# A decoder layer on one core: transposes by DMA, score maxima inside the product, two tanh gates, and every engine's order written out

## The reference

```
x = x + attention(layernorm(x))       # 16 query heads in 4 groups of 4, 4 key/value heads of 16, rope, causal softmax
x = x + cross(layernorm(x), ctx)      # scores over 256 features with ctx, mask of keys, softmax, readout of ctx
x = x + ffn(layernorm(x))             # 256 -> 2 x 704 -> 256
# ffn: every row of x, w_gate_up, h and w_down is rounded to 127 steps of its largest magnitude
gate_up = xq @ w1q.T;  h = silu(gate) * up;  y = quant(h) @ w2q.T
```

## Time and profile before

| what | value |
| --- | --- |
| median of 3 runs | 142.97 us (140.73 to 143.29) |
| span of the profiled execution | 146.3 us; the page gives no other time of that execution |
| busiest engine over the span | PE 124.6 us, 85% |
| granted TensorE clock, mean | 0.820 of full speed |
| DMA packets and bytes | 7281, 6.97 MB |

### The profile page before, as it was taken

How to read it: one execution, slowest core, us unless ns; L and a number is a source line. 1 busy time by engine, 2 the same in 40 slices (tenths; PEclk the granted TensorE clock), 3 DMA queues, 4 the chain that set the end, 5 groups by cost and what they waited for, 6 DMA issues and landing times.

```text
span 146.3 us, 2608 instructions
## 1 busy us (share of the span) xinstructions
PE 124.6 (85%) x730; PEld 95.8 (65%) x730; DVE 96.7 (66%) x392; ACT 73.3 (50%) x179; POOL 44.8 (31%) x81
## 2 busy tenths in 40 slices
PE   0899739969979999999999999679889999994770
PEld 0676527757856896858687876558777877782330
DVE  4997969754943346776767345543599999969421
ACT  4012152932645435767583635538777876683200
POOL 3405071210312210322310212130664656666111
PEclk9999995999855558999999555557999999998555
DMA  1799801010010002010101010100000011001211
GB/s 51 189 347 331 309 1 40 0 36 0 0 36 4 2 2 72 2 36 0 36 0 36 4 36 6 30 0 0 0 0 7 0 36 36 23 20 36 72 36 36
DMA packets 7281, 6.97 MB, mean 48 GB/s; under 512 B 1185, under 2 KB 7014, under 8 KB 7270
## 3 DMA queue, kind: packets, MB, share of 16 engines
q1 hardware_dynamic: 7270, 6.84, 15.0%
HBM read 5.79 MB, written 1.05 MB: 47 GB/s over the span
## 4 chain that ended last, share of the span: by engine, by line
PE 63%; DVE 19%; issue 6%; ACT 4%; POOL 3%; DMA 1%; POOLq 1%; DVEq 0%; ACTq 0%; SPq 0%
PE ps_s L372 5%; PE bank L389 5%; PE bank L426 5%; PE ps_s L528 5%; PE bank L346 4%; PE bank L528 4%; PE bank L562 4%; PE bank L380 4%; PE bank L401 3%; PE bank L439 3%; PE bank L337 3%; PE bank L329 3%; POOL hid L1466 2%; PE bank L412 2%; PE bank L414 2%
## 5 line engine op out<-in xcount | busy, mean ns | idle before, releaser
L1466 POOL TENSOR_TENSOR hid<-gate,up 128x704 f32<-128x704 f32 x8 | 13.6, 1697 | 14.9 <-ACT up L808 14.9
L337 PE MATMUL bank<-causal,ident_b 128*128 128x256 bf16 x82 | 14.1, 322 | 4.2 <-DVE ident_b L916 4.1
L1434 POOL TENSOR_SCALAR w_q<-w_int,w_scale 128x256 f32<-128x256 int16 x11 | 5.2, 480 | 34.2 <-ACT w_int L726 34.2
L337 PEld LDWEIGHTS bank<-causal,ident_b 128*128 128x128 bf16 x82 | 9.2, 115 | 6.5 <-DVE ident_b L916 4.1
L562 PE MATMUL bank<-w_T,h_T 128*128 128x256 bf16 (+1 forms) x48 | 9.3, 323 | 4.1 <-DVE h_T L1246 4.0
L666 ACT COPY xn_T<-bank 128x256 f32<-128x256 f32 x8 | 3.0, 373 | 16.9 <-PE bank L321 16.9
L1425 POOL TENSOR_SCALAR ln_var<-x_sumsq 128x1 f32<-128x1 f32 x8 | 1.5, 191 | 29.2 <-ACT x_square L702 29.2
L528 PE MATMUL ps_s<-w_hi,x_int_T 128*128 128x352 f32 x32 | 9.1, 369 | 1.2 <-ACT x_int_T L792 1.2
L329 PE MATMUL bank<-ident,w_q 128*128 128x128 f32 x22 | 5.3, 330 | 5.7 <-DVE w_lo L1083 3.4
L1062 DVE SCALAR_TENSOR_TENSOR resid<-bank,c_factor,resid 128x256 f32 (+1 forms) x8 | 3.9, 484 | 9.5 <-PE bank L439 9.5
L389 PEld LDWEIGHTS bank<-v_ones,p_self_T 128*128 128x128 f32 x64 | 9.9, 230 | 0.3 <-issue 0.3
(11 more groups left out here) (149 smaller groups left out, 340.8 us busy)
## 6 DMA issues: line engine op xcount, KB each, us to landing
x_in<-in_x SPq DMA_DIRECT2D x8, 128.0 KB, 2.2
resid<-in_x SPq DMA_DIRECT2D x1, 1024.0 KB, 7.6
ctx_sb<-in_ctx SPq DMA_DIRECT2D x8, 128.0 KB, 2.1
out_x<-resid SPq DMA_DIRECT2D x8, 128.0 KB, 1.7
w_raw<-in_L_ffn_w_gate_up SPq DMA_DIRECT2D x1, 896.0 KB, 8.3
w_raw<-in_L_ffn_w_down SPq DMA_DIRECT2D x1, 704.0 KB, 8.3
w_raw<-in_L_ffn_w_gate_up SPq DMA_DIRECT2D x1, 512.0 KB, 4.4
wq_raw<-in_L_attn_Wq SPq DMA_DIRECT2D x1, 256.0 KB, 2.6
```

The source lines that it names most:

```text
L337: nc.tensor.matmul(ps_xc[:, 0:2 * T], ident_b[:, :], causal[:, :, :], start=True, stop=True)
L1466: nc.gpsimd.tensor_tensor(hid[par][:, :].rearrange("p (i f) -> p i f", i=2), gate[par][:, :, :], up[par][:, :, :], ALU.mult).then_inc(s["h ...
```

## The change

The kernel is written anew, with the same arithmetic in its outline. What is different:

- **Layout.** The host lays out x, its transpose, the context and its transpose, weights and rope tables by partition (`laid_out`: reshapes, transposes, copies of constants). The transposes of x (L321) and of the context (L414) fall away. SP and ACT issue the loads.
- **Norm 1 is folded into weights.** The mean is subtracted from the weights' columns (`mean_w_first`, `centre_w_first`), and the row factor r1 multiplies after the product, so x itself is the operand. The bias is added after rope on POOL (`rope_bias`, `rotate_c`, `rotate_sum`), while DVE does one operation per batch (`rotate`).
- **Maximum in the product.** Scores are computed once to find the row maxima (`scores`, `max_scores`); the negated maximum is written beside the 16 features of q as a 17th, q is transposed again (`transpose_q_max`), and a second set of products (`score_keys`) gives scores less the maximum, already transposed. Exponentials are taken from PSUM; POOL sets later keys to 0 (`drop_later_keys`). The transposes of probabilities (L380) and the subtraction (L998) fall away.
- **Values in column tiles.** Four products of 32 output rows each with the probabilities as moving operand (128 columns), and four more with ones for the sums (`weigh_values`); the result is already transposed.
- **Integers for up.** The up half stays in integers (one part, 4 products instead of 8); its scale is a row that POOL multiplies into the gate (`widen_gate`). The gate half keeps two parts, and its lower part is made by POOL (`lower_gate`).
- **Transposes by DMA.** w1, w2, x of batches 0 to 5 and h of batches 0 to 2 are transposed as 2-byte numbers by DMA from SP. The others go through TensorE.
- **Gate by tanh for batches 0 and 1** (`tanh_gate`, `finish_gate` on DVE), silu for the others.
- **Cross bias on POOL** (`bias_cross`), context centred on POOL (`centre_ctx`).
- **The end.** The last batch is cut in halves (`last_gate` to `last_down_b`).
- **All orders laid out.** No loops or slots: one list of steps for each engine. After the start no `keep_warm` is left (54 in all, 82 before).

```diff
-                nc.vector.tensor_reduce(s_negmax[:, :].rearrange("p (b h) -> p b h", b=2), scores, AX.X, ALU.max, negate=True).then_inc(s["negmax_done"], 1)
-                nc.vector.tensor_tensor(by_bank(s_shifted[:, :, :]), scores, by_bank(broadcast(s_negmax[:, :], T)), ALU.add).then_inc(s["shifted_ready"], 1)
-                    last = nc.tensor.transpose(ps_p[:, h * T:(h + 1) * T], p_self[par][:, h, :], ident[:, :])
-                    last = nc.tensor.matmul(ps_y[:, h * (DH + 1):(h + 1) * (DH + 1)], p_self_T[:, h, :],
-                                            v_ones[par][:, h, :], start=True, stop=True)
+                    nc.tensor.matmul(ps_s[:, h, 0:T], qk_T[j % 3][h * HP:h * HP + DH, 0, :],
+                                     qk_T[j % 3][h * HP:h * HP + DH, 1, :], start=False, stop=True).then_inc(s["scores_done"], 1)
+                nc.vector.tensor_reduce(qk_rot[j % 3][:, 0, :, DH], ps_s[:, :, 0:T], AX.X, ALU.max, negate=True).then_inc(s["negmax_done"], 1)
+                nc.tensor.transpose(ps_qm, qk_rot[j % 3][:, 0], ident[:, :]).then_inc(s["q_max_transposed"], 1)
+                    nc.tensor.matmul(ps_s[:, h, 0:T], qk_T[j % 3][h * HP:(h + 1) * HP, 1, :],
+                                     q_max_T[j % 3][h * HP:(h + 1) * HP, :], start=True, stop=True).then_inc(s["keys_done"], 1)
+                nc.scalar.activation(p_self_T[j % 3][:, :, :], ps_s[:, :, 0:T], ACT.Exp).then_inc(s["p_T_ready"], 1)
+                    nc.tensor.matmul(ps_yv[h * HP:(h + 1) * HP, :], v_pad[:, j, h, :], p_self_T[j % 3][:, h, :],
+                                     start=True, stop=True, tile_position=(0, h * HP)).then_inc(s["y_done"], 1)
+                    nc.tensor.matmul(ps_ys[h * HP:(h + 1) * HP, :], ones[:, :], p_self_T[j % 3][:, h, :],
+                                     start=True, stop=True, tile_position=(0, h * HP)).then_inc(s["y_done"], 1)
+                nc.vector.reciprocal(y_rsum[j % 3][:, :], ps_ys).then_inc(s["y_rsum_done"], 1)
...
-                nc.gpsimd.tensor_scalar(w1_q[par][:, :], w1_int[par][:, :], w1_scale[par][:, 0:1], 1.0,
-                                        ALU.mult, ALU.mult).then_inc(s["w1_q_ready"], 1)
-                    last = nc.tensor.transpose(ps_lnw[:, D + c * P:D + (c + 1) * P],
-                                               w1_q[par][:, c * P:(c + 1) * P], ident[:, :])
+                sp.dma_start_transpose(w1_T[:, 0:GT + 1, :, :].rearrange("p o c t -> p (o c) t"),
+                                       w1_int[:, 0:GT + 1, :].rearrange("p o d -> p (o d)")).then_inc(s["gate_T_loaded"], 16)
+                sp.dma_start_transpose(x_T[:, j, :, :], x_int[:, j, :]).then_inc(s[f"x_T_{j}_loaded"], 16)
+                sp.dma_start_transpose(h_T[j % 2][:, :, :], h_bf[j % 2]).then_inc(s[f"h_T_{j % 2}_loaded"], 16)
...
-                    last = nc.scalar.copy(up[par][:, i, :], ps_up[i][:, 0:FH])
-                nc.gpsimd.tensor_tensor(hid[par][:, :].rearrange("p (i f) -> p i f", i=2), gate[par][:, :, :], up[par][:, :, :],
-                                        ALU.mult).then_inc(s["hid_ready"], 1)
+                nc.gpsimd.tensor_tensor(gate_up[j % 2][:, :, :], gate[j % 2][:, :, :], up_row.rearrange("p (i f) -> p i f", i=2),
+                                        ALU.mult).then_inc(s["gate_up_ready"], 1)
+                nc.vector.scalar_tensor_tensor(hid[j % 2][:, :, :], ps_s[:, 2:4, 0:FH], scale, gate_up[j % 2][:, :, :],
+                                               ALU.mult, ALU.mult).then_inc(s["hid_ready"], 1)
+                nc.scalar.activation(gate[j % 2][:, :, :], ps_s[:, 0:2, 0:FH], ACT.Tanh, scale=x_half[:, j:j + 1]).then_inc(s["tanh_done"], 1)
+                nc.scalar.mul(ffn[j % 3][:, :], ps_y[:, 0:D], h_scale[:, j:j + 1]).then_inc(s["down_scaled"], 1)
```

More of the change, by code:

```diff
@@ new lines, in decoder_layer @@
+        gate = [gates[:, i] for i in range(2)]
+        gate_T = [gates[:, c].rearrange("p i f -> p (i f)") for c in range(DC)]
+        gate_row = hid[1][:, :, :].rearrange("p i f -> p (i f)")
+        w2_bf = padded[:, 0:DC]
+        h_bf = [padded[:, DC + i] for i in range(2)]
+        x_T = w2_raw[:, :, :].rearrange("p c f -> p (c f)")[:, 0:X_BY_DMA * D // 2].bitcast(I16).rearrange("p (j c t) -> p j c t", c=DC, t=T)
+        w1_scale = w_scale[:, 0:WT]
+        w2_scale = w_scale[:, WT:WT + DC]
@@ L313, in _ @@
+            store_out(4)
+            store_out(5)
+            store_out(6)
+            store_out(7)
+            sp.wait_ge(s["out_stored"], 16 * B)
         @block.tensor
         def _(pe):
-            def transpose_xn1(half, u):
-                k, par, n = at(half, u, 0)
-                free(pe, "w1_lo_ready", max(2 * k - 1, 0) if type(k) is int and k < 4 else k + 3)
-                done(pe, "xn1_ready", k)
-                for c in range(DC):
-                    last = nc.tensor.transpose(ps_lnw[:, c * T:(c + 1) * T], xn1[par][:, c * P:(c + 1) * P], ident[:, :])
-                last.then_inc(s["xn1_transposed"], 1)
@@ new lines, in product, with gate_free @@
+            def product(j, first, parts, signal):
+                for c in range(DC):
+                    for w in parts:
+                        for i in range(2):
+                            last = nc.tensor.matmul(ps_s[:, first + i, 0:FH], x_int_T[:, j, c, :], w[:, c, i * FH:(i + 1) * FH],
+                                                    start=c == 0 and w is parts[0], stop=c == DC - 1 and w is parts[-1])
+                last.then_inc(s[signal], 1)
+            def gate_free(j):
+                if 1 <= j <= EARLY:
+                    pe.wait_ge(s["early_gate_ready"], j)
+                elif j > EARLY:
+                    pe.wait_ge(s["gate_ready"], j - EARLY)
@@ L632, in _ @@
-            pe.wait_ge(s["w2_diag_ready"], 1)
-            for c in range(DC):
-                last = nc.tensor.matmul(ps_w2[c][:, W2_ROW:W2_ROW + P], ones[:, :], w2_diag[:, c, :], start=True, stop=True)
-            last.then_inc(s["w2_transposed"], 1)
-            filling_slot(1, 1, (0, 1, 2, 3), [(5, 1), (6, 0)])
-            pe.wait_ge(s["valid_ready"], 1)
-            with pe.Fori(2, B // 2) as half:
-                for u in (0, 1):
-                    attention_slot(half, u, tiles=[(2 * half + u + 3, 1 - u)])
@@ new lines, in last_down_b @@
+            def last_down_b():
+                done(pe, "last_h_T_b_ready", 0)
+                for f in range(FC // 2, FC):
+                    n = P if f < FC - 1 else FL
+                    last = nc.tensor.matmul(ps_y[:, 0:D], h_T[LAST % 2][0:n, f, :], w2_T[0:n, f, :],
+                                            start=False, stop=f == FC - 1)
+                last.then_inc(s["down_done"], 1)
+            pe.wait_ge(s["const_set"], SET["warm"])
+            keep_warm(30); mean_w_first(); keep_warm(6); bias_wo(); keep_warm(2); project(0); keep_warm(11)
@@ L894, in _ @@
-            nc.vector.memset(big_row[:, :], -MASKED).then_inc(s["const_ready"], 1)
-            nc.vector.memset(pow_exp[:, :], -0.5).then_inc(s["pow_exp_ready"], 1)
-            nc.vector.memset(y_aug[:, :], 1.0)
-            nc.vector.memset(qk_rot[:, :, :, :], 0.0)
-            for i in range(2):
-                last = nc.vector.memset(v_ones[i][:, :, :], 1.0)
-            last.then_inc(s["zeros_ready"], 1)
-            def stats_1(first, n, count):
+            nc.vector.memset(warm[:, :], 0.0).then_inc(s["const_set"], 1)
```

2049 lines of the change are left out of this document (912 added, 1137 removed).

## The result

The changed kernel takes **96.52 us** (median of 4 runs, 95.91 to 96.94), the kernel before 143.13 beside it (4 runs, 140.73 to 149.21): a ratio of 0.681, 95% interval 0.674 to 0.688. The profiled execution took 96.81 us, its span is 95.1. Executions of one kernel differ in the clock that TensorE was granted: the ratios leave out the long ones, and the profiled execution of the kernel before (clock 0.820, span 146.3) is itself a long one, where 23 of the 36 executions beside the later runs have a clock of 0.869 to 0.889 and a span of 138.7 to 141.7.

The account below looks back on a forecast made before the run. TensorE, part of the time at half clock, was taken to bound the kernel. Start 10.5 + 7 periods of 7.6 + 3 + remainder 48.5 gave 115.2 us of span, times 0.977 a forecast of 113 us; 8-in-10 range 100 to 129.

Parts of the forecast that it names:

- start and weight maxima: Before the first scores 10.5 us, plus 3 us in the first periods for the maxima of w1 and w2.
- seven periods: From the first to the last batch's scores: seven attention periods of 7.6 us each, at 34% half clock.
- remainder: From the last batch's scores to the end: 43.5 us with TensorE at 90%, then 5 uncovered, 48.5 in all.
- a period on TensorE, "No overlap shows": One attention period: 7.35 us at full clock without tile overlap, 6.45 taken with values and sums at 0.9.
- The clock: TensorE in attention periods: 34% of the time at half clock, the share of before; 6.45 us full, 11.4 half.
- The factor 0.977: Whole kernel: median time 142.97 over span 146.3 of before, turning 115.2 us of span into 112.6 of time.
- The quick rival: Attention tiles overlap wholly: ACT bounds a period, 6.7 us; time 104, or 100 at full clock throughout; chance 0.15.
- Start: Loads and the weights' path up to the first scores: 10 to 11 us, taken as 10.5.
- Transposes by DMA: Rival in the feed-forward: they come late, at 5 us each, or POOL blocks a ready step; time 121, chance 0.11.
- The slower rival: All of attention at half clock without tile overlap: 12.9 us a period, time 150; chance 0.04.
- POOL and DVE: Beside TensorE: POOL about 65 us, hidden unless ahead of a ready step; DVE some 3.5 a period plus reciprocal 0.8.

Follow-up runs that it names:

- a_pairs: Changed kernel with its first score products issued in pairs as before, the last two heads each waiting for an earlier one: 97.77 us.
- b_warm: Kernel before with four bf16 products of 256 columns added behind the value products: 137.57 us, ratio 0.966.
- a_rowserial: Changed kernel with each head of both score products waiting for the head before it, so row tiles can't overlap: 149.46 us, ratio 1.036.
- a_short: Changed kernel with 19 keep-warm products for 30 and 3 for 6 at the start, first projection ahead of the bias product: 96.57 us against 96.89.
- a_later: Changed kernel with the first gate product and ACT's copy of the first rounded x moved behind later attention steps: 99.38 us.
- a_dve: Changed kernel with the lower gate and the cross bias on DVE instead of POOL: 96.18 us, ratio 0.679.
- a_best: Changed kernel with the moves of a_later, the shorter start filling of a_short, and lower gate and cross bias on DVE: 96.61 us.
- a_colserial: Changed kernel with each of the four value products and four sums waiting for the one before, so column tiles can't overlap: 117.94 us, ratio 0.829.
- a_cold: Changed kernel without its 54 keep-warm products: 104.26 us, ratio 0.736.

## Why the prediction was wrong

The direction and the way of dividing the time were right. On the profiled spans 115.2 was forecast and 95.1 measured, 20.1 less. By the prediction's own terms: start and weight maxima 13.5 forecast, 14.1 measured (+0.6); seven periods 53.2 and 36.2 (-17.0); remainder 48.5 and 44.8 (-3.7). Two small slips of the sum change little: 7.35 less 1.76 plus 0.9 is 6.49 (6.45 taken), and 39.6 less 0.9 at 90% is 43.0 (43.5 taken).

- **The step that failed: a period on TensorE, "No overlap shows".** I read L372's 1.04 us as eight tiles in series, at 0.13 each. It is two overlapping pairs with a wait between them, as a_pairs shows by giving 1.07 to the same tiles in the changed kernel. The wait stood in the code of before (head_scored) and as idle time by L372 itself. With the measured 0.50, 0.50 and 0.57 in place of 1.04, 1.04 and 1.76 the count of 7.35 becomes 5.08, and 5.17 is measured, with TensorE busy 4.84 of it. The other terms held in sum and not one by one: the projection takes 0.65 from start to start for 0.85, and the means of the context (32 products, 4.6 us of records) were not counted at all. Against the 6.45 taken the period is 9 us shorter in seven. The Trainium skill ("TensorEngine Tiling (Array Packing)", Tiling Modes, and "TensorE: Matmul & The Clock Gate", Part 3) says that different tiles can run at the same time, and I set it aside for L372's sake. The trace agrees in kind: four row tiles take 0.50 us where one alone takes 0.48 and four in series 2.11.
- **The clock.** I took over the 34% of half clock from before, for a kernel with other products, and from an execution with less clock than most (0.820 for 0.869 to 0.889). It was 0%, worth 8 us in the seven periods. b_warm shows that fillers end most of before's half clock, a_rowserial that the changed kernel falls to half clock when the row tiles wait. What I named for the low clock, that fillers are dropped, didn't come about. TensorE is busy 94% of the periods, but a_rowserial at 92% shows that this alone doesn't explain it.
- **From span to time.** The factor 0.977 divides the median of three executions by the span of one that was longer than they were. In the 36 listed executions of the kernel before the time is 2.1 to 2.3 us above the span, in the changed kernel 1.7, so 115.2 of span stood for some 117 us of time. The forecast of 113 came 4 us nearer to the result by this error.
- **The quick rival** had the mechanism (tiles overlap wholly, 0.15) and gave 100 at full clock. It missed the rest because it let ACT bound a period with 5.6 us; ACT is busy 27.25 us in seven periods, 3.9 each. Rounding and copying of weights are 10.0 of records there, for 11.9 forecast. The rest is smaller because only five cross exponentials and nine of the squares fall into these periods, and because records of ACT overlap: all groups of the stretch together are 32.7 us.
- **Remainder.** 38.7 us of TensorE at 90% and 5 of drain were forecast; measured are 34.84 busy of 39.0 and 5.8 of drain. The share was right (89%), the work nearly 4 us too large; which products account for that no run shows.
- **Start.** 10.5 was too early by 3.6: thirty keep-warm products hold TensorE until 7.11 us, 1.6 after the summed weights are there, and more stand ahead of the first projection. I had costed the weights' path and not TensorE's own queue. The 3 us for the maxima of the weights didn't show as a longer period. By a_short the fillers cost the kernel nothing: what is saved there ends in a wait 40 us later.
- **Transposes by DMA** were in time: 2.3 to 3.6 us, and no gate waited for one in the changed kernel. The margin is thin. One took 4.0 in a_short and then set the gate's start.
- **The slower rival** (half clock throughout and tiles in series, 150 us) resembles what a_rowserial built, at 149.5. Its condition, little but half clock in attention, was met there and not in the changed kernel. That the two numbers agree is in part luck: the rival priced a group in series at 1.04 us (1.8 at half clock), and the groups of a_rowserial take 2.11 and 3.33, while its column tiles still overlap.
- **POOL and DVE.** 65 us forecast for POOL, 66.3 measured. It is hidden from TensorE's row, but not off the path: 32% of the last chain is POOL's, and in a_later POOL's queue, with another step ahead of a ready bias, is behind the 1.75 us of idle time; that was named among the rivals. Reciprocal 0.8 forecast, 0.953 measured. DVE comes to 4.6 us a period for my 4.3, so it is now the engine next to TensorE. On the port pair that the Trainium skill ("SBUF — State Buffer", SBUF: two separate sides) names, no run isolates a cost; a_dve, which takes two kinds of steps off POOL, changes nothing.

What stays open: which property of TensorE's work holds the clock. Row tiles in series lose it, and column tiles in series, with seven waits a batch for six, keep it at 0.991. After an idle piece of 1.75 us (a_later) it fell for about a slice, after 1.37 (a_short) and 1.29 (a_best) it did not. Open too is how the time saved divides between the tiles, the clock and the products that are gone.

## What to carry to other kernels

A group's time over its count is the speed of an instruction only if nothing waits inside the group: read the code between two products before taking a rate from them. A granted clock of before belongs to the order and the products of before, and to one execution: give a change that replaces them its own clock, let the range hold both, and compare the span that you divide by with the spans of other executions. An early gain is lost where a later step waits for something that didn't come earlier (a_short); move a step only after asking which wait it covers (a_later).

## What the runs showed of the hardware

- Four row tiles of 16 or 32 rows take 0.50 us together and one alone 0.48. With a semaphore wait before each of the last three they take 2.11 at full clock and 3.33 at half: each wait costs 0.54 us at full clock, more than the whole group (a_rowserial).
- Four column tiles of 32 columns, 128 float32 columns through each, take 0.24 to 0.33 us from start to start; in series by waits 1.80 (a_colserial).
- TensorE can count as busy for 92% of a span and run at half clock for half of it (a_rowserial), with the same products that run at full clock when no wait stands between them.
- More products on the bounding engine made a kernel 3.4% faster [1.8, 5.0], with the mean clock at 0.951 for 0.873 to 0.885 (b_warm).
- A page can show a granted clock of 1.000 where the same products take twice as long as later: projections of 1.60 us at 20 us and of 0.82 at 40 (a_cold). The durations of a repeated product tell more there.
